# A ring of gathered rows eight groups deep instead of four, and one-hots four groups ahead, in a four-layer graph network

## What is computed

```python
# layer 0: one matrix per edge type (16)
msg = h[src] @ W0[edge_type_16];           x = x + segment_sum(msg, dst)
# layer 1: mean of the sources
mean = segment_sum(h[src], dst) / max(count, 1)
x = x + elu(mean @ W_l.T + b_l + h @ W_r.T)
# layer 2: a message network with edge attributes
m = silu(concat(h[src], h[dst], edge_attr) @ w1 + b1) @ w2 + b2
x = x + layernorm(h + silu(concat(h, segment_sum(m, dst)) @ w3 + b3) @ w4 + b4)
# layer 3: attention over 4 rules, one matrix per edge type (8), softmax within each destination
x = x + relu(layernorm(segment_sum(h[src] @ Wr[edge_type_8] * attn, dst) + bias))
```

## Time and profile before

| | us |
|---|---|
| median of 3 runs (2767.8 to 2774.67) | 2771.57 |
| the profiled execution, its own time | 2766.72 |
| its span, first to last instruction | 2764.9 |
| POOL busy | 1613.2 (58%) |
| PE busy | 1369.1 (50%) |
| DVE busy | 739.2 (27%) |

### The profile page before, as it was taken

The page is one execution under the profiler, slowest core; times in us unless marked ns, Lnnn a source line. Parts: engine busy times, 40 slices in busy tenths (PEclk is TensorE's granted clock), DMA queues, the critical chain, the costliest instruction groups (busy, mean ns, idle before and its releaser), DMA issues.

```text
span 2764.9 us, 21557 instructions
## 1 busy us (share of the span) xinstructions
PE 1369.1 (50%) x5982; PEld 1261.2 (46%) x5982; DVE 739.2 (27%) x2312; ACT 159.8 (6%) x286; POOL 1613.2 (58%) x1693
## 2 busy tenths in 40 slices
PE   6332333333332423233577777677663245655585
PEld 3232323333332323233567777676542235655585
DVE  5211111112311111113222222222421133343456
ACT  3000000000000000001000000000210000000000
POOL 2676666664766667663566666666046666656440
PEclk9555555555555555555655555555655555555555
DMA  6511111111111111110322222222052222222110
GB/s 225 159 25 22 25 23 25 22 24 27 23 24 23 24 23 24 22 25 13 64 57 55 56 57 57 57 57 52 28 219 69 68 61 66 69 57 69 46 46 12
DMA packets 159055, 144.96 MB, mean 52 GB/s; under 512 B 109905, under 2 KB 111855, under 8 KB 158802
## 3 DMA queue, kind: packets, MB, share of 16 engines
q0 software_dynamic: 53888, 69.64, 11.9%
q1 hardware_dynamic: 105058, 73.94, 9.4%
HBM read 113.55 MB, written 37.28 MB: 55 GB/s over the span
## 4 chain that ended last, share of the span: by engine, by line
POOL 28%; another core or an unknown queue 22%; issue 19%; PE 12%; DVE 10%; SPq 7%; DMA 2%; ACT 0%; DVEq 0%; ACTq 0%; POOLq 0%
POOL flat L450 28%; SPq L392 6%; PE ps L1165 3%; PE ps L1156 3%; DVE oh L785 2%; PE ps L1016 2%; DMA table<-flat 1%; DVE ohT L622 1%; PE ps L1003 1%; DVE oh L616 1%; PE ps L1113 1%; PE ps L986 1%; DVE msg L777 1%; PE ps L977 1%
## 5 line engine op out<-in xcount | busy, mean ns | idle before, releaser
L450 POOL DMA_INDIRECT flat<-table,flat x1248 | 1192.9, 956 | 706.6 <-issue 361.1
L1016 PE MATMUL ps<-flat,oh 128*128 128x65 f32 (+1 forms) x1664 | 375.3, 422 | 800.0 <-DVE oh L616 506.0
L1016 PEld LDWEIGHTS ps<-flat,oh 128*128 128x128 f32 x1664 | 360.8, 331 | 814.3 <-issue 814.3
L616 DVE TENSOR_SCALAR oh<-iota_n,drel 128x128 f32<-128x128 f32 x1248 | 261.3, 299 | 1411.8 <-remote 1104.6
L450 POOL DMA_INDIRECT uvT<-table,idx x416 | 405.3, 974 | 330.8 <-issue 122.0
L1156 PE MATMUL ps<-qn,ohT 128*128 x832 | 188.5, 413 | 186.0 <-DVE ohT L622 93.3
L1156 PEld LDWEIGHTS ps<-qn,ohT 128*128 128x128 f32 x832 | 181.7, 325 | 193.5 <-issue 193.4
L1016 PE MATMUL ps<-msg,oh 128*128 128x64 f32 x832 | 186.3, 405 | 140.7 <-issue 113.9
L1165 PE MATMUL ps<-flat,oh 128*128 128x65 f32 x832 | 192.0, 410 | 98.4 <-issue 71.6
L1016 PEld LDWEIGHTS ps<-msg,oh 128*128 128x128 f32 x832 | 179.0, 320 | 135.2 <-issue 135.0
L1165 PEld LDWEIGHTS ps<-flat,oh 128*128 128x128 f32 x832 | 186.4, 329 | 98.8 <-issue 98.7
(11 more groups left out here) (245 smaller groups left out, 722.4 us busy)
## 6 DMA issues: line engine op xcount, KB each, us to landing
table<-flat SPq DMA_DIRECT2D x52, 512.0 KB
drow<-slot_node SPq DMA_DIRECT2D x104, 256.0 KB
flat<-table,flat POOLq DMA_INDIRECT x1248
flat<-edge_attr_padded SPq DMA_DIRECT2D x416, 16.0 KB
uvT<-table,idx POOLq DMA_INDIRECT x416
edge_attr_padded<-edge_attr SPq DMA_DIRECT2D x1, 6250.0 KB
xs<-x SPq DMA_DIRECT2D x1, 768.0 KB
flat<-L_gnn_weight SPq DMA_DIRECT2D x2, 256.0 KB, 3.9
```

The lines of the kernel that those rows point to most:

```text
L450: nc.gpsimd.indirect_dma_start(dest[:, b, j, :], None, table, at_).then_inc(gat[b], 16)
L616: last = V.tensor_scalar(oh[:, b, j, :], iota_n[:], drel[:, bass.ds(g * SG + j, 1)], None, ALU.is_equal)
L1016: last = T.matmul(acc[:, bass.ds(n[j] * pitch + shift, width)], oh[:, b, j, :], rows_[:, j, :], start=False, stop=True, skip_group_check=True)
```

## The change

All three rings become eight groups deep. `got0` and `got1` now lie on one piece of memory (layer 1 starts after layer 0 is through), and `got3` moves from `uvT` to the end of the large buffer `flat`, where weights of earlier layers lie in its last part; so POOL waits at group `HELD3` (6) until these are no longer read. In layers 0 and 1 the one-hots have four buffers, made of `oh` and `ohT`, and DVE waits for group g-4 instead of g-2. Layers 2 and 3 keep two one-hot buffers. The count that `landed` waits for is written for a ring that doesn't divide 52. `TWICE = 4` keeps the layer-3 schedule as it was.

```diff
-        RING = 4
-        got0 = early(P, [RING, SG, W])
-        got1 = early(P, [RING, SG, D])
-        got3 = uvT[:, 0:RING * SG * 2 * D].rearrange("p (b s d) -> p b s d", b=RING, s=SG)
-        oh = sb("oh", [P, 2, SG, P])
+        RING, AHEAD_OH = 8, 4
+        ring = early(P, [RING * SG * W])
+        got0 = ring.rearrange("p (b s d) -> p b s d", b=RING, s=SG)
+        got1 = ring[:, 0:RING * SG * D].rearrange("p (b s d) -> p b s d", b=RING, s=SG)
+        FREE3 = 2 * P * W + 2 * P * NR
+        got3 = flat[:, FREE3:FREE3 + RING * SG * 2 * D].rearrange("p (b s d) -> p b s d", b=RING, s=SG)
+        oh_all = sb("oh_all", [P, AHEAD_OH, SG, P])
+        oh = oh_all[:, 0:2]
+        ohT = oh_all[:, 2:4]
...
-            eng.wait_ge(gat[b], (l * NB + 1) * PER + (g - b) * (PER // RING))
+            eng.wait_ge(gat[b], PER * (l * len(range(b, G, RING)) + g // RING + 1))
...
-                if g == RING - 1:
+                if g == HELD3:
                     pool.wait_ge(s("node_mm"), 20)
+                    pool.wait_ge(s("qn"), 3)
...
             def simple_loop(l):
                 for g in range(G):
-                    dve.wait_ge(s("used"), l * G + g + 1)
-                    onehots(g, g % 2)
+                    if l * G + g >= AHEAD_OH:
+                        dve.wait_ge(s("used"), l * G + g - AHEAD_OH + 3)
+                    onehots(g, g % AHEAD_OH)
...
                     if l == 0:
-                        sum_into_nodes(b % 2, n, got0[:, b], PITCH, SHIFT, W)
+                        sum_into_nodes(g % AHEAD_OH, n, got0[:, b], PITCH, SHIFT, W)
```

More of the change, by code:

```diff
@@ L218, in network @@
         PAIRS = ("wk1", "w1a", "w1b", "w3a", "wq", "wl", "wr", "w23", "w4", "centre")
-        paired = early(P, [len(PAIRS), P])
-        wqk = early(P, [2 * NR])
-        bqk = early(P, [NR])
         b23 = early(P, [D])
@@ L225, in network @@
         pre2 = early(P, [NT, D])
+        late = taken[0]
+        paired = early(P, [len(PAIRS), P])
+        wqk = early(P, [2 * NR])
+        bqk = early(P, [NR])
+        HELD3 = (late - FREE3) // (SG * 2 * D)
         HALVES = ((0, 16), (16, NT))
@@ L261, in network @@
         INIT, INIT_W = 5, 4
-        NB = G // RING
-        assert G % RING == 0
         def group_of(engine, row_, g, largest):
@@ L283, in landed @@
         def landed(eng, l, g, b):
-            eng.wait_ge(gat[b], (l * NB + 1) * PER + (g - b) * (PER // RING))
+            eng.wait_ge(gat[b], PER * (l * len(range(b, G, RING)) + g // RING + 1))
         BIG, FAR = 1e38, 2.0 ** 20
+        TWICE = 4
         def chunk(eng, c, step):
             for lg in range(PIECES[c]):
-                step(FIRST[c] + lg, lg, lg % RING, PIECES[c] - lg)
+                step(FIRST[c] + lg, lg, (FIRST[c] + lg) % RING, PIECES[c] - lg)
         def summed(c, lg, left):
@@ L299, in summed @@
                 return [lg]
-            once = PIECES[c] - RING
+            once = PIECES[c] - TWICE
             return [FIRST[c - 1] + lg] if lg < once else [FIRST[c - 1] + once + 2 * (lg - once) + k for k in range(2)]
-        assert PIECES == (16, 16, 12, 8) and sum(PIECES) == G and SC == 4 and RING == 4
+        assert PIECES == (16, 16, 12, 8) and sum(PIECES) == G and SC == 4 and TWICE == 4
         NW = 0
@@ L615, in onehots @@
                 for j in range(SG):
-                    last = V.tensor_scalar(oh[:, b, j, :], iota_n[:], drel[:, bass.ds(g * SG + j, 1)], None, ALU.is_equal)
+                    last = V.tensor_scalar(oh_all[:, b, j, :], iota_n[:], drel[:, bass.ds(g * SG + j, 1)], None, ALU.is_equal)
                 last.then_inc(s("oh"), 1)
@@ L792, in step @@
                     for k, w in enumerate(summed(c, lg, left)):
-                        weights_of(w, b if c < 2 or left > RING else k)
+                        weights_of(w, b if c < 2 or left > TWICE else k)
                     score(g, lg, b)
@@ L1015, in sum_into_nodes @@
                 for j in range(SG):
-                    last = T.matmul(acc[:, bass.ds(n[j] * pitch + shift, width)], oh[:, b, j, :], rows_[:, j, :], start=False, stop=True, skip_group_check=True)
+                    last = T.matmul(acc[:, bass.ds(n[j] * pitch + shift, width)], oh_all[:, b, j, :], rows_[:, j, :], start=False, stop=True, skip_group_check=True)
                 last.then_inc(s("used"), 1)
@@ L1174, in step @@
                     for k, (w, n_w) in enumerate(earlier):
-                        weigh(w, w if c < 3 else w - 2 * PIECES[0], b if c < 2 or left > RING else k, n_w)
+                        weigh(w, w if c < 3 else w - 2 * PIECES[0], b if c < 2 or left > TWICE else k, n_w)
                 return step
```

4 lines of the change are left out of this document (2 added, 2 removed).

## The result

The changed kernel takes 2839.52 us (median of 4, 2830.65 to 2850.73), the kernel before beside it 2773.12. The ratio is 1.0244, 95% interval [1.0203, 1.0285]. I had 2735 and a range up to 2792. The profiled execution has a span of 2834.8 us, 69.9 more than before. From its page: the span, the engines, POOL's gathers of layers 0 to 2 and PE's sums of layers 0 and 1 (busy and mean ns of one | idle before, and its largest share).

The account below looks back on a forecast made before the run. POOL's gathers bound the kernel, with PE's signals late during unbroken bursts. Layers 0 and 1 -37 and -34, their ends +7 each, layers 2 and 3 +10 each: -37 us, giving 2735 us, range 2675 to 2792.

Parts of the forecast that it names:

- The sum's base: Whole kernel: the profiled execution's 2766.7 us, with the median of the runs shown 4.9 us higher.
- the ends of layers 0 and 1: After the last gather: 2 to 3 groups left to PE, +7 us a layer, 0 to 14.
- (52 - 9) / 7 gives 6 pauses of 5.7 us: Layers 0 and 1: longer bursts leave 34 us of POOL pauses a layer, for 71.0 and 68.5.
- the -37 and -34 us: Layers 0 and 1: time saved by fewer POOL pauses; bounds -25 and -23 to -71 and -68.
- d + 4 groups: Layers 0 and 1: burst length, d being signals arriving in it; 7 or 8 groups expected, 6 at worst.
- Layer 2: Late start +23, faster end -16, same rate of 11.8 us a group; +10 us taken, from -16 to +21.
- Layer 3: Longer first burst delays chunk 0 some 20 us, faster end -16; +10 us taken, bounds -16 and +30.
- My -16 for the end: End of layer 3: four more groups run without POOL, priced as in layer 2, saving 16 us.
- The slower one (2, at 2803): Starts of layers 2 and 3: long bursts starve the chains, +31 us, 2803; chance 0.18.
- Rival 1: Layers 0 and 1: signals also arrive after 40 us, pauses nearly vanish; typically -105 us, 2667; chance 0.17.
- Rival 4, the port: Layers 0 and 1: one-hots wait for POOL's shared port, not `used`; -30 and -28 us, 2747; chance 0.05.
- That the two sides cancel (3): Whole kernel: bursts of 6 and half of the late starts cancel within 0.3%; 2768 us; chance 0.1.

Follow-up runs that it names:

- e17: Changed kernel plus a 128-column POOL memset behind each gather: 2850.23 us beside 2775.76, ratio 1.0272.
- e18: Changed kernel plus a 224-column POOL memset behind each gather: 2753.93 us beside 2771.66, ratio 0.9932.
- e5: The changed kernel itself, unaltered, on a chip without pauses: 2386.94 us beside 2387.07, ratio 1.0000.
- e1: Changed kernel with POOL waiting for group g-4 in all four layers, on a chip without pauses: 2383.31 us beside 2384.43.
- e4: Changed kernel with POOL four groups ahead in layers 0 and 1, eight in 2 and 3, on a chip without pauses: 2383.66 us beside 2384.43.
- e7: Changed kernel plus 800 small SyncE DMAs in layer 0: 2827.35 us beside 2754.34, ratio 1.0268.
- e8: Changed kernel plus 800 small SyncE DMAs in layer 0, POOL waiting for group g-4: 2759.31 us, ratio 1.0006.
- e16: Changed kernel, POOL waiting for group g-4 and, before each group's fourth gather, for the group before to land: 2772.43 us beside 2767.33, ratio 0.9998.
- e3: Changed kernel with POOL eight groups ahead in layers 0 and 1, four in 2 and 3, on a chip without pauses: 2382.88 us beside 2384.43.
- e2: Changed kernel with DVE waiting for group g-2 in layers 0 and 1, on a chip without pauses: 2382.92 us beside 2384.43.
- e11: Changed kernel with half of PE's sums in layers 0 and 1 left out: 2809.05 us beside 2772.73.

## Why the prediction was wrong

**What held.** On the chip of the result signals of PE come late while POOL gathers without a break, POOL and DVE wait for `used`, and the first burst grows to ten groups. The sum's base and the ends of layers 0 and 1 (+12.6 and +5.8 for a +7 each, bounds 0 to 14) are about as I had them.

**The step that failed** is "(52 - 9) / 7 gives 6 pauses of 5.7 us", in both of its factors. There were 13 pauses a layer, most of them after four groups, so the -37 and -34 us became -0.5 and +0.2 in the loops; this is 71 of the 107 us between the forecast sum of -37 and the trace's +69.9. And the price was wrong too. I took 5.7 us for a stop, whatever the burst before it, because nearly all pauses in the earlier trace rows followed bursts of four groups. The price goes by what was gathered: the one long burst of layer 0 was followed by 12.9 us, and over a loop the pauses sum to 64 to 73 us however they are cut (and with a gap after each gather they go, e17 and e18). So at this price fewer pauses would hardly have saved anything either. The number was within reach: 5.59 us after 40 in the earlier trace rows, but I had read it as a delay after the stop ("once POOL stops they all come within about 5 us") and not as 0.14 for each microsecond gathered.

**The burst after the first** was to be d + 4 groups, "one signal in 22 us to 30 us". I had counted on PE taking up the four groups of one-hots during the burst. In fact it slows to a record in 1.4 to 2.8 us, and in a cycle of layer 0 it finishes three groups just after POOL's stop (564.0 to 570.8), the fourth at 577.7 and none until 609.4. The bursts stayed at four groups with eight buffers; whether for PE's crawl or for the late signals no run separates. I had written that pauses after every four groups would mean that `used` is not what POOL waits for. That inference was wrong too: by the kernel POOL waits for `used`, of a group that PE had finished 38 us before.

**Layer 2**: +10 forecast, +16.3 measured. What held is the rate, 11.8 us a group from the ninth on. What was mis-sized is the late start. The changed kernel (start, us; idle before):

```profile
1430.40 1.68 DVE L622 TENSOR_SCALAR oh_all<-iota_n,drel 128x128 f32<-128x128 f32 x8 [46.46 <-remote]
1430.63 0.95 POOL L455 DMA_INDIRECT flat<-table,flat  x1 [9.62 <-remote]
```

The ninth group starts 90.7 us into the loop, and it needs the first group summed, as the fifth did before at 52.0: the chain is 38.7 us late, where I took +23 and had 37 for the case that nothing gets through. The last eight groups then saved 21 where I took 16, although I had misread their price: POOL still gathers until 1937.6 in the earlier trace rows, so the part with POOL silent is 20.5 us for three groups, 6.8 each.

**Layer 3**: +10 forecast, +36.6 measured, over my bound of +30. Here too it is the late start. The changed kernel takes up the second and third group of scores so:

```profile
2138.87 0.19 DVE L783 COPY rule_e<-ps 128x32 f32<-128x32 f32 x1 [41.96 <-remote]
2178.76 0.19 DVE L783 COPY rule_e<-ps 128x32 f32<-128x32 f32 x1 [37.72 <-remote]
```

The third begins 110 us into the loop; before it was 59. Chunk 0 is scored 34 us later than before (I took some 20), chunk 1 51 later, where I had put nothing, and the last group 36.5 later; from there to the end it is 64.4 us in both traces. My -16 for the end was about right (50 late after chunk 2, 36.5 at the end). Seen from POOL, which had run ahead, the same lateness stands behind its last gather as the ends of the table.

**The rivals.** The slower one (2, at 2803) had the side and the place right: late starts of 25 us or more in layers 2 and 3, and a loss there (21 and 30 forecast, 16.3 and 36.6 measured). What it had wrong is the gain of 20 in layers 0 and 1, which lose 18.1. Rival 1 fell with the pauses, which stayed. Rival 4, the port, would have DVE write one-hots only while POOL stands or just after; DVE's row at 531.96 above lies 14 us into a burst, and in layers 0 and 1 of e18 POOL doesn't stand at all. That the two sides cancel (3) is what the times show wherever the lead was four.

**The scope.** The loss belongs to the chips on which before takes 2754 to 2776, five in these runs beside that of the result. On four others it takes 2384 to 2388, POOL never pauses, and the change is worth nothing in either direction (e5). What e1 to e4 were to tell apart was told by e5, e7, e8 and e16. The kernels with a long lead in two layers alone (e3, e4) and with one-hots two ahead (e2) were not run on a chip with pauses; the split by layer rests on the three pairs of traces. In all three layer 3 loses most, 34 to 37 us, and layers 0 and 1 lose 6 to 14 each.

## What to carry to other kernels

A deeper ring helps when the consumer is late now and then; when the producer itself slows the consumer, the lead only becomes work left over at the end of each loop, and the longer first burst holds up the chain behind it; so count what stands behind the last transfer, and what waits during the first burst, before deepening one. Plot a pause against the burst before it before taking its length as fixed: a price for each burst and a price for each item look alike as long as all bursts are equal. And where an engine is idle "issue" with its operands ready, compare the same instruction in a quiet stretch; if the kernel's time differs by a sixth from one chip to the next, find out which kind of chip a change is for.

## What the runs showed of the hardware

- One program, two speeds, and it goes with the chip: 2384 to 2388 us for the kernel before on four chips, 2754 to 2776 on five and in the result, with TensorE's mean granted clock 0.53 on both. The gathers' instructions (0.95 us) and DVE's one-hots (1.66 us for eight) are the same; what differs is when PE's and SyncE's instructions run and when PE's signals arrive, while POOL issues gathers one in 1.25 us. With one in 1.42 us the difference goes in layers 0 and 1, but not in layer 2. (In e18 the eight one-hots take longer, 345 ns each against 299, beside POOL's memsets.)
- Signals of PE were 38 us late in the cycle of the result shown above and 51 in e11, by PE's own records; those of landed gathers were not late. PE's records in the crawl start some 0.7, 1.4, 2.1 or 2.8 us apart, multiples of what one of SyncE's issues takes there (0.70 us, one in 1.40).
- How much the other engines do hardly matters to the sum of the pauses: half of PE's records and 800 DMAs of SyncE left layer 0 at 585.7 to 589.3 us.
- The traces of the slow chips list fewer semaphore updates of the same program: 9,512 in the result, 14,761 in e18, 38,264 in e5. The record of events thins out on the chips where signals are late. The Trainium skill (page "NOTIFIC — the notification-queue block", section "7.1 Overflow: three behaviours, one of which stalls the engine") says that the block which writes such records holds its producers back when its own pipeline fills, and its section "10. Constraints, capacities, measured rates" that emitting a record costs an engine no cycles. Engines that are held back would fit the first; missing records would not, since the page has that stall in place of a loss. If this block is the path, the crawl of PE speaks against the second as a general rule. No run here shows that it is, and the gathers, not the instructions, set the pile. Every time in this document was taken with such records, so whether the two speeds exist without them is not shown. What the path is stays open.
